# A two-layer graph network on one core: the first round of each half B goes from VectorE to ScalarE, with an accumulator of its own that GpSimd joins

## The chip, the core and the metric

One core of one Trainium2 chip. A core has TensorE (PE: matmuls, with its weight loads, PEld), VectorE (DVE), ScalarE (ACT), GpSimd (POOL) and SyncE (SP), which here only issues DMAs. Each engine works through its own queue in program order and waits on semaphores. PSUM has eight banks of 512 float32 in each of 128 partitions. The metric is the device time of one execution in microseconds; lower is better.

## The reference

128 graphs of 128 nodes with 64 features. Layer 0 is an edge network: for each node the sum over its neighbours of a ReLU of a 192-wide vector, then a 192x64 product. Layer 1 is a message layer with a GRU. Both are residual and end in a layer norm.

```python
def _L0_gnn_ref(x, adj, W1, b1, W2, b2):
    mask = (adj > 0.0)
    W1a, W1b = (W1[:F], W1[F:])
    diff = x[:, :, None, :] - x[:, None, :, :]
    h = relu((x @ W1a)[:, :, None, :] + diff @ W1b + b1)
    hm = jnp.einsum('bjkh,bjk->bjh', h, mask)
    return hm @ W2 + deg[..., None] * b2

x = _layernorm(x + L0(x, adj))
# L1: m = relu(relu(h W1 + b1) W2 + b2); msg = relu(A m); GRU(msg, h)
x = _layernorm(x + L1(x, adj))
```

## The kernel before, in words

**The sum over neighbours.** The adjacency is sparse, so layer 0 is not computed edge by edge over all 128 x 128 pairs. Each node gets its neighbours one after another: in a *round*, TensorE adds into PSUM, for every node of four graphs at once, a matmul with a one-hot matrix (float8 pieces cut out of the bit table `CW`) that swaps the previous neighbour's vector for the next one's. VectorE then reads the three banks, takes the ReLU and adds it to the accumulator `AC`, all in one SCALAR_TENSOR_TENSOR (`max 0, add AC`). The neighbours are in two halves, A (nodes with low numbers, weights `VA`) and B (`VB`). Each half has nine rounds. Rounds 1 to 6 cover 192 columns for each of six tiles (1152 elements), rounds 7 and 8 cover 128 (768 elements), round 9 covers 80 (480 elements). The columns beyond the 128 nodes hold nodes with more neighbours than nine; half A uses the left 64 of them, half B the right 64, and both halves share the middle 128 of one `AC` tile (4 tiles of 128x256 and 2 that hold the rest of the 192 hidden units).

**Turns.** Four graphs make one group `q` (32 groups). In *turn* `t` the program issues, for n from 1 to 9, `round_b(t-1, n)` and then `round_a(t, n)`: half B of the older group alternates with half A of the newer one. Banks 0 to 2 hold even groups, 3 to 5 odd ones, so group t can only be seeded when half B of group t-2 has been read for the last time. So a turn begins with this chain: last B round of group t-2 read by VectorE, `seeds(t)` on TensorE (L836 and L842, it starts PSUM with the node's own term), `seeds(t)` on ScalarE (L1525, ReLU of it into `AC`), `seeds(t)` on GpSimd (L1745, times the number of surplus slots `NNB`), and `round_a(t, 1)` on VectorE, which adds to that `AC` (it waits for `im` and for the cleared outer columns, `clr`).

**The first B round.** `round_b(q, 1)` on TensorE waits for the last A round of group q (`sx`), takes the last A neighbour out again (`leave`, 8 matmuls of 128 columns, L850 and L858) and then adds the first B neighbour (8 matmuls of 192 columns). VectorE reads it like any other round.

**What else the engines do in a turn.** `dgen(t, 0..3)` on VectorE cuts the four one-hot sources `DM[m]` out of `CW` (L1138, 16-bit shifts in SBUF); `words` (L1128) makes the table of the next group; `off` (L1119) every second turn. `prep` (ranks, tables, transposed x, `v`, `surplus` which is ScalarE's `NNB` copy L1513 and L1516), `tail(q)` (`s_ov`, `out0_a`, `out0_b`, `out0_c`: the product with W2 and the residual) and layer 1 (`layer1_steps`) fill TensorE, ScalarE and GpSimd between rounds. GpSimd has the mask (L1698), `gt`, `gt_in`, `gd`, `h` of the GRU (L1640 to L1664), the differences to a float16 copy (L1710 to L1734), the powers of the norms, and `clear` (L1738).

**The order.** The strings `ORDER[t % 2]` (`FIRST` for turn 0, `LAST` for the two last turns) say which step goes between which rounds, for all engines at once: string 2n-1 stands between B round n and A round n, string 2n between A round n and B round n+1, string 0 ahead of B round 1. The letters: `s` seeds, `0` `1` dgen of the next turn, `2` `3` dgen of this turn, `p` prep, `t` tail of group t-2, `r` ranks, `e` `d` `n` layer 1, `c` clear, `l` load. The order within each engine's queue follows from it.

## Time and profile before

| | us |
|---|---|
| three runs | 879.21, 876.65, 873.9 |
| median | 876.65 |
| the profiled execution, its own time | 877.91 |
| span of its trace | 876.3 |
| mean granted TensorE clock | 0.984 of full speed |

Between the span and the execution's own time lie 1.6 us. "Busy" is the union of an engine's instructions. Ends of matmuls are modelled, so that a busy TensorE isn't always one at its peak. "Idle before, released by" is time in which an engine had nothing to run, with the event that ended it. From turn 4 or so to turn 31 the trace repeats itself every two turns within some 0.1 us.

### The profile page before, as it was taken

What the parts mean: (1) busy time and instruction counts of PE and PEld (TensorE: products, weight loads), DVE (VectorE), ACT (ScalarE), POOL (GpSimd) and SP (SyncE); (2) the same over time, 40 slices, a digit from 0 to 9 for tenths busy, and PEclk for the clock granted to TensorE, in tenths of its full rate; (3) what the DMA queues carried; (4) which work ended last, traced back from release to release, by engine and by line L of the source; (5) the groups of instructions that cost most, each with busy time, mean ns of one, the idle gap of its engine ahead of it and who ended that gap; (6) DMA issues with size and microseconds to landing.
All of it is one profiled execution on the core that took longest, in us unless ns stands there. A gap on an engine that the chain in (4) does not pass through costs nothing.

```text
span 876.3 us, 25828 instructions
## 1 busy us (share of the span) xinstructions
PE 786.3 (90%) x10335; PEld 651.6 (74%) x10368; DVE 803.6 (92%) x880; ACT 606.7 (69%) x1863; POOL 462.1 (53%) x536
## 2 busy tenths in 40 slices
PE   3777889999999999999999999999999999999873
PEld 2556677778887787878787787888778787877752
DVE  6799999999999999999999999999999999998961
ACT  4534465777777777777877777787777777776552
POOL 5412243474737547383746647473755738363661
PEclk9998999999999999999999999999999999999996
DMA  3423132322223132313213232312313231221000
GB/s 121 111 46 87 26 92 55 91 54 85 54 65 91 29 104 56 104 32 100 59 33 98 56 103 56 90 46 72 87 27 104 56 104 33 67 56 38 1 13 26
DMA packets 31564, 57.55 MB, mean 66 GB/s; under 512 B 8273, under 2 KB 8913, under 8 KB 31441
## 3 DMA queue, kind: packets, MB, share of 16 engines
q1 hardware_dynamic: 31440, 55.86, 24.5%
q8 instruction: 83, 1.36, 0.6%
q14 instruction: 41, 0.33, 0.1%
HBM read 13.90 MB, written 4.19 MB: 21 GB/s over the span
## 4 chain that ended last, share of the span: by engine, by line
PE 51%; issue 28%; DVE 16%; ACT 2%; POOL 1%; DMA 1%; SPq 1%; POOLq 0%; DVEq 0%
PE PS L850 12%; PE PS L858 11%; DVE AC L1182 8%; DVE AC L1162 4%; PE PS L836 2%; PE PS L932 2%; PE PS L920 2%; PE PS L677 2%; PE PS L842 2%; PE PS L666 2%; PE PS L617 1%; PE PS L618 1%; PE PS L620 1%; PE PS L629 1%; PE PS L627 1%
## 5 line engine op out<-in xcount | busy, mean ns | idle before, releaser
L1182 DVE SCALAR_TENSOR_TENSOR AC<-PS,AC 128x1152 f32<-128x1152 f32 (+2 forms) x279 | 329.4, 1181 | 26.6 <-PE PS L850 25.1
L1162 DVE SCALAR_TENSOR_TENSOR AC<-PS,AC 128x1152 f32<-128x1152 f32 (+2 forms) x279 | 329.4, 1180 | 4.9 <-PE PS L858 2.9
L850 PE MATMUL PS<-DM,VA 128*128 128x192 fp8e5 (+1 forms) x1024 | 121.5, 241 | 17.2 <-DVE AC L1162 11.1
L858 PE MATMUL PS<-DM,VB 128*128 128x192 fp8e5 (+1 forms) x1024 | 120.6, 240 | 17.9 <-DVE AC L1182 15.0
L850 PE MATMUL PS<-DM,VB 128*128 128x192 fp8e5 (+1 forms) x1024 | 119.8, 240 | 0.5 <-DVE AC L1179 0.5
L858 PE MATMUL PS<-DM,VA 128*128 128x192 fp8e5 (+1 forms) x1024 | 120.3, 240 | 0.1
L850 PEld LDWEIGHTS PS<-DM,VA 128*128 128x128 f16 x1024 | 77.7, 99 | 47.8 <-DVE AC L1162 30.4
L1745 POOL TENSOR_TENSOR AC<-AC,NNB 128x512 f32<-128x512 f32 x64 | 66.1, 1053 | 85.7 <-DVE DM L1138 51.4
L858 PEld LDWEIGHTS PS<-DM,VB 128*128 128x128 f16 x1024 | 75.6, 98 | 43.4 <-issue 18.8
L858 PEld LDWEIGHTS PS<-DM,VA 128*128 128x128 f16 x1024 | 83.5, 98 | 0.9 <-DVE AC L1159 0.6
L850 PEld LDWEIGHTS PS<-DM,VB 128*128 128x128 f16 x1024 | 83.4, 98 | 0.9 <-DVE AC L1179 0.9
L1138 DVE TENSOR_SCALAR DM<-CW 128x1536 uint16<-128x1536 uint16 (+1 forms) x132 | 79.2, 628 | 2.5 <-DMA CW<-WM 2.5
L1738 POOL MEMSET AC<- 128x768 f32 x32 | 23.6, 739 | 66.9 <-PE PS L949 66.2
L1698 POOL TENSOR_SCALAR MT<-AT 128x1024 bf16<-128x1024 f32 x15 | 42.1, 2808 | 24.2 <-DMA AT<-in_adjt 23.9
L1734 POOL TENSOR_TENSOR SHL<-SO,SHL 128x256 f16<-128x256 f32 x31 | 28.5, 918 | 49.7 <-ACT SHL L1533 49.7
L1506 ACT ACTIVATE VN<-PS 128x384 f16<-128x384 f32 x64 | 31.2, 487 | 30.5 <-PE PS L815 30.0
L1495 ACT ACTIVATE XE<-PS 128x512 f16<-128x512 f32 x64 | 37.7, 591 | 19.1 <-PE PS L789 19.1
L1501 ACT ACTIVATE VN<-PS 128x384 f16<-128x384 f32 x64 | 31.7, 496 | 20.9 <-PE PS L809 19.3
L1540 ACT ACTIVATE XR<-PS 128x256 f32<-128x256 f32 x32 | 12.3, 384 | 48.5 <-PE PS L949 48.5
L1430 ACT ACTIVATE YO<-Y,st 128x64 f32<-128x64 f32 x120 | 31.8, 337 | 16.3 <-POOL st L1633 16.3
L1475 ACT ACTIVATE AM<-PS 64x512 int16<-64x512 f32 x64 | 37.7, 589 | 6.1 <-PE PS L757 5.7
L1128 DVE TENSOR_TENSOR WM<-c,AM 128x1280 uint16<-128x1280 uint16 x32 | 39.7, 1240 | 2.0 <-ACT OT L1489 2.0
(266 smaller groups left out, 2077.5 us busy)
## 6 DMA issues: line engine op xcount, KB each, us to landing
CW<-WM SPq DMA_DIRECT2D x128, 160.0 KB, 2.8
AT<-in_adjt SPq DMA_DIRECT2D x16, 512.0 KB, 4.9
VA<-VN SPq DMA_DIRECT2D x64, 128.0 KB, 2.3
VB<-VN SPq DMA_DIRECT2D x64, 128.0 KB, 2.3
XN<-in_xn SPq DMA_DIRECT2D x16, 256.0 KB, 4.8
out<-YO SPq DMA_DIRECT2D x15, 256.0 KB, 2.9
cs<-in_cst SPq DMA_DIRECT2D x1, 544.5 KB, 3.4
out<-YO SPq DMA_DIRECT2D x2, 128.0 KB, 1.7
```

The source lines that it names most:

```text
L850: last = e.matmul(PS[:, b + i % 2, 256 * (i // 2) + cols.start:256 * (i // 2) + cols.stop], left(lhs, i), d[:, i, :], start=False, stop=Tr ...
L858: last = e.matmul(PS[:, b + 2, 256 * (i // 2) + cols.start:256 * (i // 2) + cols.stop], right(lhs, i), d[:, i, :], start=False, stop=True, ...
L1128: e.tensor_tensor(WM[q % 2][:], c7[:], AM[q % 2][:].bitcast(U16), ALU.logical_shift_left).then_inc(s["wm"], 1)
L1138: e.tensor_scalar(DM[m][:, halves], CW[t % 3][:, halves, first], 6 - 2 * m, 0xC0C0, ALU.logical_shift_left, ALU.bitwise_and).then_inc(s["d ...
L1162: e.scalar_tensor_tensor(dst, tiles(PS[:, b:b + 3, :])[:, :, cols], 0.0, dst, ALU.max, ALU.add).then_inc(s["sx"], 1)
L1182: e.scalar_tensor_tensor(dst, tiles(PS[:, b:b + 3, :])[:, :, cols], 0.0, dst, ALU.max, ALU.add).then_inc(s["sy"], 1)
L1430: last = e.activation(YO[:, k, :], Y[:, k, :], ACT.Copy, scale=st[:, 3, k:k + 1])
L1475: e.activation(graphs(am[k])[:, :, 64 - 64 * h:192 - 64 * h], src[k], ACT.Copy, scale=2.0, bias=-258.0)
L1495: e.activation(XE[q % 4][:, 2 * k:2 * k + 2, :].rearrange("p i n -> p (i n)"), PS[:, b, :], ACT.Copy).then_inc(s["xe"], 1)
L1501: e.activation(VN[q % 2][:, 0, k:4:2, 0:H], PS[:, b, :].rearrange("p (a n) -> p a n", a=2)[:, :, 0:H], ACT.Copy).then_inc(s["vh"], 1)
L1698: e.tensor_scalar(MT[g % 3][:], AT[g % NA][:], 0.0, None, ALU.is_gt).then_inc(s["mask"], 1)
L1745: e.tensor_tensor(t[:, h, nat], t[:, h, nat], NNB[q % 2][:, h, :], ALU.mult).then_inc(s["im"], 1)
```

## The change

1. VectorE no longer does `round_b(q, 1)`. ScalarE does: one ACTIVATE Relu over the 1152 elements (two, of 384 and 768, for the last group), which *writes* an accumulator of half B of its own, `BB[q % 2]`. VectorE's B rounds 2 to 9 add to `BB`. One `BB` is new memory, the other lies over the constants that are not needed after the start (`cs`, whose `CSL` column moves forward for that).
2. GpSimd gets `join(q)`: two TENSOR_TENSOR adds (128x512 and 128x256 float32) of the middle columns of `BB` to `AC`, as the first step of `tail(q)`. It waits for both halves' ninth round; `out0_a` on TensorE waits for it.
3. `clear` writes 128x384 instead of 128x768, since half B's outer columns are written and not added to.
4. `VA` has two buffers instead of three; SP's `v_out(q)` waits for the first B round of group q-2 on TensorE.
5. The tables `ORDER`, `FIRST` and `LAST` are drawn anew. Around the start of a turn the order is then:

```
even turn, before: B9 A9 dgen0 dgen1 surplus seeds dgen2 ov B1 rank_t A1 rank_ov gt_in dgen3 tanh gd B2
even turn, after:  gt_in dgen1 surplus rank_n A9 seeds ov tanh B1 gd dgen2 dgen3 A1 join rank_t h rank_ov B2
                   (dgen0 three rounds earlier, between A6 and B7)
odd turn, before:  B9 dgen0 A9 off dgen1 surplus seeds dgen2 B1 ov dgen3 m2 rank_t A1 s_ov B2 A2 msg split_ms B3
odd turn, after:   B9 dgen0 dgen1 A9 off surplus seeds B1 dgen2 msg split_ms A1 B2 ov gate_h gate_i dgen3 rank_t A2 join B3
```

```diff
-    ("s2p", "p", "pe3ee", "td", "erp", "t", "tt", "rpr", "p", "ed", "p", "epree", "pee", "d", "pce", "", "", "0", "r1"),
-    ("s2", "p3dp", "t", "", "d", "p", "eptp", "e", "ptl", "tp", "ndcpn", "d", "p", "dr", "pnd", "", "dd", "d", "01p"),
+    ("spe", "e23", "tpep", "", "tp", "rdd", "tp", "t", "ept", "rp", "erepe", "d", "p", "epce", "d", "", "de", "01", "r"),
+    ("s", "2d", "", "pdd3p", "t", "te", "p", "tp", "tt", "ndnl", "drc", "pp", "dd0p", "", "pp", "p", "d", "d1per", ""),
...
-        VA = [sb(f"VA{i}", [128, 4, 256], F16) for i in range(3)]
+        VA = [sb(f"VA{i}", [128, 4, 256], F16) for i in range(2)]
...
-        AC = [sb(f"AC{i}", [128, 3, 512]) for i in range(3)]
+        AC = [sb(f"AC{i}", [128, 6, H]) for i in range(3)]
+        BB = [sb("BB0", [128, 6, H])[:], cs[:, CTR:CTR + 6 * H].rearrange("p (k n) -> p k n", k=6)]
...
             def tail(q):
+                do("join", q)
+                yield
...
             def out0_a(q, b, gates):
-                pe.wait_ge(s["sy"], 9 * q + 9)
+                pe.wait_ge(s["jn"], 2 * q + 2)
```

On VectorE:

```diff
             def round_b(q, n):
+                if n == 1:
+                    return
```

On ScalarE:

```diff
+            def round_b(q, n):
+                if n > 1:
+                    return
+                b, dst = 3 * (q % 2), BB[q % 2]
+                ac.wait_ge(s["jn"], 2 * (q - 2) + 2)
+                ac.wait_ge(s["sov"], q - 1)
...
+                ac.wait_ge(s["gy"], 9 * q + 1)
+                e.activation(dst, tiles(PS[:, b:b + 3, :])[:, :, back], ACT.Relu).then_inc(s["sy"], 1)
```

On GpSimd, and at the end on SP:

```diff
+            def join(q):
+                po.wait_ge(s["sx"], 9 * q + 9)
+                po.wait_ge(s["sy"], 9 * q + 9)
+                for h in (slice(0, 4), slice(4, 6)):
+                    t = AC[q % 3][:, h, nat]
+                    e.tensor_tensor(t, t, BB[q % 2][:, h, 0:128], ALU.add).then_inc(s["jn"], 1)
...
             def clear(q):
                 po.wait_ge(s["o0"], q - 2)
-                e.memset(outer(tiles(AC[q % 3][:])), 0.0).then_inc(s["clr"], 1)
+                e.memset(AC[q % 3][:, :, 0:64], 0.0).then_inc(s["clr"], 1)
...
             def v_out(q):
+                sy.wait_ge(s["gy"], 9 * (q - 2) + 1)
```

## Rows read from the trace of the kernel before

**Rows 1.** The page: busy time of each engine over the span.
```profile
PE 786.3 (90%) x10335; PEld 651.6 (74%) x10368; DVE 803.6 (92%) x880; ACT 606.7 (69%) x1863; POOL 462.1 (53%) x536
```
**Rows 2.** Busy time by stretch: an even turn, then an odd one.
```profile
423.69:448.34 24.65, 22.74 (x316) 19.11 (x316) 24.65 (x25) 19.31 (x61) 18.19 (x25) 1.00 0.21 50
448.34:473.65 25.31, 25.15 (x331) 20.95 (x332) 23.47 (x25) 18.78 (x58) 11.20 (x10) 1.00 0.33 90
```
**Rows 3.** Groups by line and form: busy us, mean ns of one, idle before.
```profile
L1182 DVE SCALAR_TENSOR_TENSOR AC<-PS,AC 128x1152 f32<-128x1152 f32 x186 | 250.8, 1348 | 23.3 <-PE PS L850 21.9
...
L1745 POOL TENSOR_TENSOR AC<-AC,NNB 128x512 f32<-128x512 f32 x32 | 43.9, 1372 | 85.7 <-DVE DM L1138 51.4 <-ACT AC L1525 34.3
...
L1495 ACT ACTIVATE XE<-PS 128x512 f16<-128x512 f32 x64 | 37.7, 591 | 19.1 <-PE PS L789 19.1
...
L1516 ACT ACTIVATE NNB<-PS 64x256 f32<-64x256 f32 x64 | 23.9, 373 | 0.4
...
L1745 POOL TENSOR_TENSOR AC<-AC,NNB 128x256 f32<-128x256 f32 x32 | 23.5, 733 | 0.0
```
**Rows 4.** VectorE in order of time (start, us) around an even turn's start.
```profile
419.89 0.65 DVE L1182 SCALAR_TENSOR_TENSOR AC<-PS,AC 128x480 f32<-128x480 f32 x1
...
421.18 1.51 DVE L1138 TENSOR_SCALAR DM<-CW 128x1536 uint16<-128x1536 uint16 x3
423.69 1.36 DVE L1182 SCALAR_TENSOR_TENSOR AC<-PS,AC 128x1152 f32<-128x1152 f32 x1 [0.99 <-PE PS L850]
424.97 1.36 DVE L1162 SCALAR_TENSOR_TENSOR AC<-PS,AC 128x1152 f32<-128x1152 f32 x1
426.24 0.55 DVE L1138 TENSOR_SCALAR DM<-CW 128x1536 uint16<-128x1536 uint16 x1
426.71 1.35 DVE L1182 SCALAR_TENSOR_TENSOR AC<-PS,AC 128x1152 f32<-128x1152 f32 x1
```
**Rows 5.** TensorE in order of time at the same place: seeds, leave, B1.
```profile
420.63 0.60 PE L836 MATMUL PS<-XE,wxh 128*128 128x256 f16 x4
...
421.83 0.39 PE L842 MATMUL PS<-XE,wxl 128*64 128x256 f16 x4
422.38 0.39 PE L850 MATMUL PS<-CW,VA 128*128 128x128 fp8e5 x4 [0.16 <-DVE DM L1138]
...
423.16 0.49 PE L850 MATMUL PS<-DM,VB 128*128 128x192 fp8e5 x4
```
**Rows 6.** ScalarE in order of time at the same place.
```profile
422.10 0.87 ACT L1525 ACTIVATE AC<-PS 128x512 f32<-128x512 f32 x2
422.86 0.69 ACT L1465 ACTIVATE OV<-PS,cs 128x512 bf16<-128x512 f32 x1
```
**Rows 7.** GpSimd in order of time at the same place.
```profile
417.30 2.79 POOL L1698 TENSOR_SCALAR MT<-AT 128x1024 bf16<-128x1024 f32 x1 [1.00 <-DMA AT<-in_adjt]
...
422.87 1.96 POOL L1745 TENSOR_TENSOR AC<-AC,NNB 128x512 f32<-128x512 f32 x2 [1.53 <-ACT AC L1525]
```
**Rows 8.** VectorE in order of time around the next odd turn's start.
```profile
444.64 0.64 DVE L1182 SCALAR_TENSOR_TENSOR AC<-PS,AC 128x480 f32<-128x480 f32 x1
...
449.61 1.04 DVE L1138 TENSOR_SCALAR DM<-CW 128x1536 uint16<-128x1536 uint16 x1
450.57 1.34 DVE L1162 SCALAR_TENSOR_TENSOR AC<-PS,AC 128x1152 f32<-128x1152 f32 x1
452.28 1.36 DVE L1182 SCALAR_TENSOR_TENSOR AC<-PS,AC 128x1152 f32<-128x1152 f32 x1 [0.36 <-PE PS L850]
```
**Rows 9.** GpSimd in order of time at that odd turn's start.
```profile
448.08 2.15 POOL L1745 TENSOR_TENSOR AC<-AC,NNB 128x512 f32<-128x512 f32 x2 [2.71 <-DVE DM L1138]
```
**Rows 10.** One line's instructions (min/median/max ns): VectorE's words.
```profile
L1128 DVE TENSOR_TENSOR WM<-c,AM x32: 810/815/1921, 19.8 to 779.3; 128x1280 uint16<-128x1280 uint16 x32
```
**Rows 11.** VectorE's words and GpSimd beside it, in order of time.
```profile
429.24 1.90 DVE L1128 TENSOR_TENSOR WM<-c,AM 128x1280 uint16<-128x1280 uint16 x1
...
429.18 1.27 POOL L1656 TENSOR_TENSOR GT<-GT,GZ 128x512 f32<-128x512 f32 x1
```

More of the change, by code:

```diff
@@ L46 @@
 CI = 0
-CTR = CI + 128
+CSL = CI + 128
+CTR = CSL + 1
 CTX = CTR + 128
@@ L293, in build @@
         ident = cs[:, CI:CI + 128]
+        ACD = [t[:].rearrange("p (a b) n -> p a (b n)", b=2) for t in AC]
         nat, front, back = slice(64, 192), slice(0, 192), slice(64, 256)
@@ L885, in round_a @@
                     pe.wait_ge(s["sx"], 9 * q + n - 1)
-                last = wide(q, VA[q % 3][:], d, cols)
+                last = wide(q, VA[q % 2][:], d, cols)
                 if q == 0:
@@ L896, in round_b @@
                     leave = lasts(q, 0, 0)
-                    wide(q, VA[q % 3][:], leave, nat)
-                    padded(q, VA[q % 3][:], leave, nat)
+                    wide(q, VA[q % 2][:], leave, nat)
+                    padded(q, VA[q % 2][:], leave, nat)
                 elif q == NQ - 1:
@@ L1562, in scalar_main @@
             follow(main_order, {"rank_n": rank_n, "split_x": split_x, "off": off, "ov": ov, "rank_t": rank_t, "rank_ov": rank_ov,
-                                "x_turn": x_turn, "v": v, "v_low": v_low, "surplus": surplus, "seeds": seeds, "s_ov": s_ov, "out0_c": out0_c,
+                                "x_turn": x_turn, "v": v, "v_low": v_low, "surplus": surplus, "seeds": seeds, "round_b": round_b, "s_ov": s_ov, "out0_c": out0_c,
                                 "fold": fold, "split_x1": split_x1, "split_h": split_h,
@@ L1750, in dgen @@
                     po.wait_ge(s["dd"], RD * t + m + 1)
-            follow(main_order, {"setup": setup, "parts": parts, "count": count, "split_x": split_x, "mask": mask, "split_xg": split_xg, "split_ms": split_ms, "split_x1": split_x1, "split_h": split_h, "s_ov": s_ov, "clear": clear, "seeds": seeds, "dgen": dgen, **gpsimd_layer1(e, po, s)})
+            follow(main_order, {"setup": setup, "parts": parts, "count": count, "split_x": split_x, "mask": mask, "split_xg": split_xg, "split_ms": split_ms, "split_x1": split_x1, "split_h": split_h, "s_ov": s_ov, "join": join, "clear": clear, "seeds": seeds, "dgen": dgen, **gpsimd_layer1(e, po, s)})
         def gpsimd_dense(e):
```

62 lines of the change are left out of this document (31 added, 31 removed), and 2 rows, old and new, of the table MAIN.

## The prediction

> **What bounds the kernel now.** I read the page first: VectorE is busy for 803.6 of 876.3 us, TensorE for 786.3, ScalarE for 606.7, GpSimd for 462.1 [rows 1]. Then the busy time of one even and one odd turn, since the trace repeats in pairs of turns. In the even turn VectorE has no idle time at all in 24.65 us; in the odd one it is busy for 23.47 of 25.31 us, while TensorE is busy for 25.15 [rows 2]. A pair takes 49.96 us, of which VectorE idles 1.84. So VectorE is the bound by its share, with TensorE close behind, and the instruction that the change takes away is one of its costliest: a round of 1152 elements, 1348 ns each [rows 3]. They overlap a little: in order of time the next one starts 1.27 to 1.28 us later [rows 4].
>
> A share doesn't say what the removal is worth. I therefore read the start of a turn in order of time, engine by engine. Call X the end of the last B round of the turn before. At the even turn X is 420.54 (419.89 + 0.65). TensorE starts the seeds at 420.63, because they need the banks that this round read [rows 5]; their last group starts at 421.83 and has 0.24 to go, and the 8 leave matmuls start at 422.38, the first B round ends its issue by 423.5. ScalarE turns the seeds into `AC` from 422.10 on, in 0.87 [rows 6]. GpSimd multiplies them from 422.87 for 1.96, until 424.83 [rows 7]. Only then may VectorE add A round 1, and it does at 424.97 [rows 4], X + 4.43. So B round 1 (423.69) stands in a gap that VectorE has anyway: the seed chain X, TensorE, ScalarE, GpSimd, A round 1 takes nearly as long without it. That is what the reader is to see: 24.65 of 24.65 busy, and yet a chain beside it that is as long as the work.
>
> At the odd turn X is 445.28 (444.64 + 0.64). GpSimd multiplies from 448.08 for 2.15 [rows 9], A round 1 starts at 450.57, X + 5.29, and B round 2 at 452.28, X + 7.00, after 0.36 of idle [rows 8]. Here the chain frees A round 1 at 450.23, X + 4.95.
>
> **The change part by part.** The paying case: 31 groups by 1.27 us is 39 us. Now what the chain leaves of it.
>
> *Even turn.* Before, B round 2 starts at X + 6.17 (426.71) [rows 4]. After, dgen 0 has left this stretch for the middle of the turn before (it will cost 0.47 there, the step from 426.24 to 426.71), and dgen 1 to 3 (3 x 0.5) and A round 9 end at about X + 2.0. Then VectorE waits for the multiplied seeds. They come at X + 4.3 if nothing moves, at about X + 4.1 if ScalarE, now done with its `NNB` copies ahead of the turn, starts them 0.3 earlier: the seeds' first half is through TensorE by X + 1.2. A round 1 then ends 1.27 later at X + 5.4. The other chain is the new one: seeds end X + 1.55, ov 0.2, leave and B1 1.1, ScalarE, then B round 2 on TensorE, 0.66 for its 8 matmuls and some 0.2 to be seen. ScalarE's read of 1152 elements isn't in the trace. Bounds: not under the 0.59 of 512 elements and, by the step from 256 (373 ns) to 512 (591 ns, both [rows 3]), 0.85 ns an element, so 1.14; at most the 1.35 that VectorE takes. I take 1.14, as the same engine's slope is the nearest row. Ahead of it in ScalarE's queue stand ov (0.69 [rows 6]) and tanh. So B round 2 is ready at about X + 5.5, and starts there: 0.67 earlier than before, less the 0.47 of dgen 0, a gain of 0.2. If ScalarE is late by half a microsecond, it is a loss of 0.3.
>
> *Odd turn.* dgen 0 and 1, A round 9, `off` and dgen 2 end near X + 3.1. The multiplied seeds come at X + 4.7 (GpSimd free of a dgen) to X + 4.95 (as now), B round 2 is 1.27 later, X + 6.0 to 6.2 against 7.00. But dgen 3, ahead of A round 1 before, now follows B round 2: 0.47, and more if GpSimd is in its way. So the gain is 0.3 to 0.5 without that wait.
>
> *GpSimd's work.* Join costs GpSimd 1.37 + 0.73 = 2.1 us a turn, by the same forms [rows 3]; half of a clear is given back. It is hidden where nobody waits: `out0_a` comes slots later. The cost lies elsewhere. words on VectorE takes 815 ns as a median and 1921 at most [rows 10]; the one of 1.90 started at 429.24, 0.06 after a GpSimd TENSOR_TENSOR of 1.27 (429.18), and had to let it end [rows 11]. dgen does so too: 1.04 beside GpSimd's second multiplication [rows 8], 0.55 alone [rows 4]. In the new odd turn `split_ms` and join stand on GpSimd just where dgen 3 is issued (seeds end X + 4.7, then 1.2 and 2.1): a wait of 0 to 1.27. I take 0.3. In the even turn words keeps a wait; its place moves, so that it costs between nothing and 1.27, before 1.09; I take 0.4 less.
> The page SBUF — State Buffer of the Trainium skill, section "SBUF: two separate sides", says that VectorE's fast forms and GpSimd share one pair of ports as an exclusive lock for a whole instruction, and the other "fully blocks". The 1.90 against 0.81 agrees; by that rule every join is a new chance for a block, and if each dgen and words met one of 0.65 the pair would lose some 3 us more, while the rounds themselves, which read PSUM, would not be touched.
>
> *Sum.* A pair gains 0.2 + 0.4 (even) and 0.4 - 0.3 (odd), 0.7 us. Turns 1 to 4 are longer by other waits; taking 15 pairs, 10.5 us. At the end of the kernel join is uncovered: nothing but the last group's product follows, so 2.1 less what runs beside it (`s_ov` and its copies), 1.5 us lost. `VA`'s new wait is free: TensorE's first B round comes at the start of the turn in which v_out is issued. 877.9 - 10.5 + 1.5 = 868.9 against the profiled execution, which is 1.26 above the median; so 868 against the median of 876.65.
>
> **The rivals.**
> *Full pay* (11%). VectorE's share decides and the tables fill the gap with other work: 31 x 1.27 = 39 us, or 30 with the end and some waits, 838 to 855. For it: no idle in the even turn. Against: the seed chain stands in the trace with its own length, and the steps that could fill the gap (dgen 0) were moved away from it.
> *Chain and TensorE eat all* (27%). The gap stays as long as it was, and in the odd turn TensorE, 25.15 of 25.31 busy, gives nothing; 0.2 to 0.3 a pair. 872.3 to 881.
> *GpSimd's queue holds the seeds* (20%). The slower side: before the even turn GpSimd runs the mask, 417.30 to 420.09, and is then free until 422.87 [rows 7] but for `gt`. The new order also puts `gt_in` (1.27, the size of row L1656 [rows 11]) ahead of the seeds' multiplication, and dgen 1 to 3 fight with it. The mask waits for a DMA, so it can't start sooner; a turn shorter by a microsecond moves X towards it. From the point at which mask, gt and gt_in (5.3 us from 417.3 on, so 422.6) end later than X + 2.0, each microsecond is one of the turn. At 0.5 to 1 us for an even turn beyond the gain, and dgen 3's full wait of 0.65 in the odd one, the pair loses 0.3 to 0.9: 881 to 892.
> That the change doesn't do what it says (ScalarE always late, so that A and B rounds lose their alternation) is the far end of the same side.
>
> **How the numbers follow.** Forecast 42%, between 855 and 872.3, likeliest 868. Full pay 11%, nothing 27%, slower 20%. 80% is reached from 852 to 884. 0.5% (4.4 us) is about what a measurement of this kernel can tell from no change. Faster by over 0.5% (under 872.3) 0.53, within 0.27, slower 0.20.
>
> **What the profile after would show.** B round 1 gone from VectorE's line and an ACTIVATE of 128x1152 at about 1.14 us. At an even turn's start VectorE idle for some 2 us, released by GpSimd's multiplication; at an odd one 1.6. B round 2 released by TensorE at X + 5.5. A pair near 49.3. words still with cases of 1.6 to 1.9, dgen more often over 1.0. If VectorE idles less than 1 us a turn and is busy about 39 us less, full pay was right. If GpSimd's L1745 group starts later than X + 2.6 in even turns, the slower rival is. The prediction falls if ScalarE's read starts far later than TensorE's B round 1 ends, or if the middle of the turns changes length by more than the two dgens.

## Result, and the profile after

| | before | after |
|---|---|---|
| median of 8 runs each, us | 876.35 | 882.83 (879.77 to 886.61) |
| after / before | | 1.0069, 95% interval 1.0048 to 1.009 |
| profiled execution, us | 877.91 | 882.54 |
| its span | 876.3 | 880.7 |
| mean granted TensorE clock | 0.984 | 0.984 |

The change made the kernel slower by 0.7%. The time was forecast at 868, faster; 882.8 lies in the range, on the other side. Ratios here and below are of runs with the chip in its faster state; one run of the second experiment was in the slower state, and its median counts it.

The page of the changed kernel, busy time of each engine (against [rows 1]):

```profile
PE 801.0 (91%) x10368; PEld 654.4 (74%) x10368; DVE 770.5 (87%) x847; ACT 643.8 (73%) x1896; POOL 520.0 (59%) x600
```

VectorE did lose its work: 803.6 became 770.5, 33 us less. ScalarE got 37 more, GpSimd 58. (TensorE, whose work is the same, reads 801.0 for 786.3; 33 of its records are missing in the trace before and its ends are modelled, so nothing is built on that.) The time didn't follow VectorE. Two turns in stretches from A round 1 to A round 1, the first mostly turn 16, an even one, the second turn 17 (columns as in [rows 2]):

```profile
426.15:451.02 24.87, 24.34 (x341) 21.02 (x342) 22.54 (x22) 21.68 (x68) 19.25 (x25) 1.00 0.21 50
451.02:475.84 24.82, 24.51 (x325) 19.48 (x323) 22.62 (x23) 18.73 (x55) 13.87 (x13) 1.00 0.34 91
```

VectorE, without any idle time in the even turn before [rows 2], now idles 2.3 us of 24.9 and 2.2 of 24.8; TensorE is at 24.3 and 24.5. Where VectorE waits, by line (busy, mean ns of one, idle before, releaser), with the groups that the change touches:

```profile
L1162 DVE SCALAR_TENSOR_TENSOR AC<-PS,AC 128x1152 f32<-128x1152 f32 x186 | 251.2, 1350 | 47.4 <-POOL AC L1767 40.9 <-PE PS L858 6.3
...
L1138 DVE TENSOR_SCALAR DM<-CW 128x1536 uint16<-128x1536 uint16 (+1 forms) x132 | 96.1, 749 | 2.9 <-DMA CW<-WM 2.9
...
L1767 POOL TENSOR_TENSOR AC<-AC,NNB 128x512 f32<-128x512 f32 x32 | 49.6, 1549 | 75.4 <-ACT AC L1524 70.1 <-DVE DM L1138 5.1
...
L1756 POOL TENSOR_TENSOR AC<-AC,BB 128x512 f32<-128x512 f32 x16 | 20.4, 1278 | 2.2 <-DVE DM L1138 2.2
```

The wait is at one place. VectorE in order of time at the start of turn 18, an even one (compare [rows 4]), and GpSimd beside it:

```profile
470.60 0.66 DVE L1181 SCALAR_TENSOR_TENSOR BB<-PS,BB 128x480 f32<-128x480 f32 x1
471.17 0.72 DVE L1138 TENSOR_SCALAR DM<-CW 128x1536 uint16<-128x1536 uint16 x1
471.81 0.64 DVE L1162 SCALAR_TENSOR_TENSOR AC<-PS,AC 128x480 f32<-128x480 f32 x1
472.37 1.52 DVE L1138 TENSOR_SCALAR DM<-CW 128x1536 uint16<-128x1536 uint16 x2
475.84 1.36 DVE L1162 SCALAR_TENSOR_TENSOR AC<-PS,AC 128x1152 f32<-128x1152 f32 x1 [1.94 <-POOL AC L1767]
477.11 1.35 DVE L1181 SCALAR_TENSOR_TENSOR cs<-PS,cs 128x1152 f32<-128x1152 f32 x1
```

```profile
470.20 1.27 POOL L1655 TENSOR_TENSOR GT<-GT,GR 128x512 f32<-128x512 f32 x1
471.64 1.38 POOL L1662 TENSOR_TENSOR GT<-GT,M 128x512 f32<-128x512 f32 x1 [0.17 <-POOL GT L1655]
473.44 2.27 POOL L1767 TENSOR_TENSOR AC<-AC,NNB 128x512 f32<-128x512 f32 x2 [0.42 <-DVE DM L1138]
```

The gap that B round 1 filled is now there to be seen: X is 471.25, A round 1 starts at X + 4.59, 1.94 of it idle. Worked out for turns 6 to 29 from VectorE's rows (12 pairs of turns; us per pair but for the first line):

| | before | after |
|---|---|---|
| one turn | 24.995 | 25.106 |
| rounds of 1152 elements | 24, 32.4 | 22, 29.7 |
| dgen, 8 | 5.00 | 6.13 |
| words, 2 | 2.67 | 2.08 |
| VectorE idle | 1.82 | 3.98 |

The rounds lost 2.6 a pair. 2.16 of idle time and 1.13 of slower dgens came back, less 0.60 of faster words. By place, with each instruction counted until the next one starts (means of the same 12 pairs, after less before, us):

| stretch | length | rounds | dgen and words | idle |
|---|---|---|---|---|
| even turn, X to B round 2 | 0.00 | -1.28 | +0.91 | +0.37 |
| even turn, the rest | +0.03 | +0.28 | -0.60 | +0.35 |
| odd turn, X to B round 2 | -0.68 | -1.34 | -0.94 | +1.58 |
| odd turn, the rest | +0.87 | -0.14 | +1.15 | -0.14 |

So the steady turns come out nearly even: the last group's B round 9 ends at 843.13 before and 843.37 after. The other 4.2 us of the span are behind it: 33.1 us from there to the end before, 37.4 after. These are single traces. A second trace of the same steady turns (the first run on the last stretch, below) has turns of 25.05 and the last round at 839.17, so 0.06 a turn, and some 4 us in the place of the last round, are not told from none. The stretch behind the last round is firmer: 33.1 to 33.3 in four traces of kernels with the structure and tables of before.

### The profile page after: what moved, and what is told of

Its sections match the earlier page's. It is cut to its first block, busy times and chain, and to the rows that moved or that the text cites. A ratio compares the mean times of both kernels' runs of the same rounds, so it can differ in the third digit from the quotient of the medians.

```text
span 880.7 us, 26002 instructions
## 1 busy us (share of the span) xinstructions
PE 801.0 (91%) x10368; PEld 654.4 (74%) x10368; DVE 770.5 (87%) x847; ACT 643.8 (73%) x1896; POOL 520.0 (59%) x600
## 3 DMA queue, kind: packets, MB, share of 16 engines
q1 hardware_dynamic: 31440, 55.86, 24.5%
## 4 chain that ended last, share of the span: by engine, by line
PE 50%; issue 17%; DVE 9%; POOL 7%; ACT 3%; DMA 1%; SPq 1%; POOLq 0%; DVEq 0%; ACTq 0%
PE PS L850 12%; PE PS L858 11%; DVE AC L1162 4%; DVE cs L1181 3%; PE PS L920 2%; PE PS L932 2%; POOL AC L1767 2%; PE PS L677 2%; PE PS L942 2%; PE PS L836 2%; PE PS L666 2%; DMA VB<-VN 1%; PE PS L939 1%; PE PS L620 1%; PE PS L618 1%
## 5 line engine op out<-in xcount | busy, mean ns | idle before, releaser
L1162 DVE SCALAR_TENSOR_TENSOR AC<-PS,AC 128x1152 f32<-128x1152 f32 (+2 forms) x279 | 329.9, 1183 | 47.7 <-POOL AC L1767 40.9
L1181 DVE SCALAR_TENSOR_TENSOR BB<-PS,BB 128x1152 f32<-128x1152 f32 (+2 forms) x128 | 149.0, 1164 | 4.0 <-PE PS L850 3.1
L1181 DVE SCALAR_TENSOR_TENSOR cs<-PS,cs 128x1152 f32<-128x1152 f32 (+1 forms) x120 | 139.6, 1163 | 6.7 <-PE PS L850 5.5
L1767 POOL TENSOR_TENSOR AC<-AC,NNB 128x512 f32<-128x512 f32 x64 | 74.9, 1189 | 75.4 <-ACT AC L1524 70.1
L1138 DVE TENSOR_SCALAR DM<-CW 128x1536 uint16<-128x1536 uint16 (+1 forms) x132 | 96.1, 749 | 2.9 <-DMA CW<-WM 2.9
L1713 POOL TENSOR_SCALAR MT<-AT 128x1024 bf16<-128x1024 f32 x15 | 43.5, 2900 | 40.9 <-DMA AT<-in_adjt 40.9
L1494 ACT ACTIVATE XE<-PS 128x512 f16<-128x512 f32 x64 | 36.1, 592 | 22.0 <-PE PS L789 22.0
L1505 ACT ACTIVATE VN<-PS 128x384 f16<-128x384 f32 x64 | 31.1, 486 | 27.1 <-PE PS L815 27.1
L1756 POOL TENSOR_TENSOR AC<-AC,cs 128x512 f32<-128x512 f32 (+1 forms) x32 | 27.4, 879 | 27.4 <-DVE DM L1138 27.3
L932 PE MATMUL PS<-w2s,AC 128*128 128x64 f32 x256 | 40.1, 289 | 0.0
L920 PE MATMUL PS<-w2s,AC 128*64 128x64 f32 x512 | 38.2, 231 | 0.0
L920 PEld LDWEIGHTS PS<-w2s,AC 128*64 128x64 f32 x512 | 33.7, 143 | 5.4 <-issue 3.8
```

The lines of the kernel that those rows point to most:

```text
L920: last = e.matmul(PS[64 * h:64 * h + 64, b, 64 * i:64 * i + 64], lhs, w2s[:, w, :], start=(w == 0), stop=(w > 0))
L932: e.matmul(o, ac[:, 2 * (i % 2) + i // 2, nat], w2s[:, 0, :], start=False, stop=True, skip_group_check=True)
L1138: e.tensor_scalar(DM[m][:, halves], CW[t % 3][:, halves, first], 6 - 2 * m, 0xC0C0, ALU.logical_shift_left, ALU.bitwise_and).then_inc(s["d ...
L1162: e.scalar_tensor_tensor(dst, tiles(PS[:, b:b + 3, :])[:, :, cols], 0.0, dst, ALU.max, ALU.add).then_inc(s["sx"], 1)
L1181: e.scalar_tensor_tensor(dst, tiles(PS[:, b:b + 3, :])[:, :, cols], 0.0, dst, ALU.max, ALU.add).then_inc(s["sy"], 1)
L1494: e.activation(XE[q % 4][:, 2 * k:2 * k + 2, :].rearrange("p i n -> p (i n)"), PS[:, b, :], ACT.Copy).then_inc(s["xe"], 1)
```

## Experiments

Ratios are to runs of the kernel before that were taken beside each experiment. "Idle" is VectorE's, us per pair of turns, worked out as above; a turn's length likewise. 

**Are the tables or the structure to blame?** First the changed kernel with all three tables of before, join right behind the seeds:

```diff
-    ("spe", "e23", "tpep", "", "tp", "rdd", "tp", "t", "ept", "rp", "erepe", "d", "p", "epce", "d", "", "de", "01", "r"),
+    ("s2p", "p", "pe3ee", "td", "erp", "t", "tt", "rpr", "p", "ed", "p", "epree", "pee", "d", "pce", "", "", "0", "r1"),
...
             def tail(q):
-                do("join", q)
-                yield
```

> The change's structure (first B round on ScalarE, own accumulator, join on GpSimd, two VA buffers) with the tables of before; join follows the seeds' multiplication at once. If the seed chain at the turn's start (last B round, TensorE, ScalarE, GpSimd, A round 1) is the reason that nothing was gained, A round 1 still starts 4.3 to 4.5 us after the last B round in even turns and near 5 in odd ones, and the time is 872 to 880. If the new tables are what spoilt the change, it is 865 or less: the removed 1.27 us a turn then shows.

Measured: 900.81, ratio 1.0288 [1.0257, 1.0319], far above the numbers of both theories; a turn 25.60, idle 5.09, A round 1 at X + 4.41 (even) and 5.87 (odd). In the even turn, with the order of before and without B round 1, A round 1 starts where it did before (4.43): this is the plainest proof that the round stood in a gap. The gap tells nothing of the rest of the turn, which grew. VectorE's waits over the run (line waited for: us, times, longest):

```profile
DVE AC L1165 <- POOL AC L1770: 33.8, 17, 2.3
DVE AC L1165 <- PE PS L861: 23.7, 30, 3.0
DVE BB L1184 <- PE PS L853: 12.3, 29, 2.1
```

Then the other half, the kernel before with only the strings of the new tables:

> The kernel before with the new tables alone; the first B round stays on VectorE, and there is no join. If the removed round only filled a gap that the seed chain leaves anyway, putting it back costs little: 880 to 888, with VectorE's wait for GpSimd's multiplication gone from about 2 us to under 1. If VectorE's work sets the time of the changed kernel, the round costs 31 x 1.27 = 39 us: about 920.

Measured: 930.45, ratio 1.0591 [1.0538, 1.0645]; a turn 26.52. Here A round 1 of even turns waits behind B round 1 and starts at X + 7.28: `DVE AC L1183 <- PE PS L851` is 49.9 us of waits. Each order is worth its time with its own structure alone. By the ratios: structure with old tables +25 us, tables with old structure +52, both +6. The new tables took back three quarters of what the structure costs in the old order.

**What join costs.** The changed kernel without it (the middle columns of half B are missing from the result):

```diff
             def tail(q):
-                do("join", q)
...
-                pe.wait_ge(s["jn"], 2 * q + 2)
+                pe.wait_ge(s["sx"], 9 * q + 9)
+                pe.wait_ge(s["sy"], 9 * q + 9)
...
-                ac.wait_ge(s["jn"], 2 * (q - 2) + 2)
```

> The changed kernel without the join: the middle columns of half B are left out of the result; out0_a waits for both halves' ninth round directly. Seed chain: join is no part of it, so 876 to 882, of which 1.5 to 3 at the end of the kernel. If GpSimd's extra 2.1 us a turn (and VectorE's short instructions waiting for it) is the cause, 868 or less.

Measured: 878.28, ratio 1.0022 [0.9996, 1.0047]; a turn 25.00, dgen 5.80, words 1.82, idle 4.28. Join is worth some 4 us (give or take 3, by the intervals). dgen and words are 0.6 a pair cheaper without it. The last stretch took 36.1 for 37.4, but that is not shown to be join's: see the end of the next part. Without join the body is as long as before, no shorter. GpSimd's busy time is back at 461.3, the 462.1 of before, and dgen keeps 0.80 of the 1.13 that the change had added: which of GpSimd's work stands beside a dgen counts for more than how much work it has.

**Is it GpSimd's multiplication?** The same kernel with the seeds not multiplied (a factor is missing), so that A round 1 waits for ScalarE's copy:

```diff
             def round_a(q, n):
-                    ve.wait_ge(s["im"], 2 * q + 2)
+                    ve.wait_ge(s["ini"], 2 * q + 2)
...
-                    e.tensor_tensor(t[:, h, nat], t[:, h, nat], NNB[q % 2][:, h, :], ALU.mult).then_inc(s["im"], 1)
```

> The changed kernel without the multiplication of the seeds on GpSimd (the surplus factor is left out of the result); A round 1 waits for ScalarE's copy of the seeds alone. Seed chain: A round 1 moves up by about 1.5 us a turn to where TensorE's A round 1 lets it start, 835 to 860. If GpSimd were not in the chain and TensorE or the middle of the turn set the time, 875 to 883.

Measured: 879.26, ratio 1.0023 [1.0002, 1.0044]; a turn 25.08, idle 4.08, A round 1 at X + 4.28 as a mean of even turns for 4.88, and 4.74 for 5.05 in odd ones. VectorE's largest wait, in the changed kernel and in this one:

```profile
DVE AC L1162 <- POOL AC L1767: 40.9, 26, 2.1
```

```profile
DVE AC L1162 <- PE PS L858: 48.3, 31, 3.0
```

The wait has the same place and about the same size, and another releaser. A chain of TensorE's (seeds, leave, B round 1, then A round 1 in its queue) stands nearly as late as GpSimd's, and the turn didn't get shorter by what A round 1 gained.

**The dgen that was moved away.** dgen 0 of odd turns goes back to the turn's end, as before the change:

```diff
-    ("s", "2d", "", "pdd3p", "t", "te", "p", "tp", "tt", "ndnl", "drc", "pp", "dd0p", "", "pp", "p", "d", "d1per", ""),
+    ("s", "2d", "", "pdd3p", "t", "te", "p", "tp", "tt", "ndnl", "drc", "pp", "ddp", "", "pp", "p", "d", "d01per", ""),
```

> The changed kernel with one step moved in its tables: the even turn's first dgen goes back from between A round 6 and B round 7 of the turn before to behind its last B round, so that it may fill VectorE's wait at the turn's start. If that wait is free room, 0.47 us are saved in every second turn: 7 us, 874 to 877. If the dgen, there, makes GpSimd's multiplication of the seeds later (GpSimd is held until it is done) or A round 9, the gain is eaten: 880 to 887.

Measured: 882.15, ratio 1.0044 [1.0024, 1.0064]; a turn 25.09, idle 3.01 and dgen 7.16. Idle time fell by 0.97 a pair and dgen rose by 1.03 (3.00 and 7.27 in a second trace with the same order): the gap can be filled, but what fills it stands beside GpSimd's work and takes the time that it frees.

**Seeds ahead of `gt_in`.** On top of the last one, `gt_in`, `tanh` and `gd` of even turns go behind B round 1 (the letter `d` of `gt_in` leaves the odd string):

```diff
-    ("spe", "e23", "tpep", "", "tp", "rdd", "tp", "t", "ept", "rp", "erepe", "d", "p", "epce", "d", "", "de", "01", "r"),
+    ("sp", "eee23", "tpep", "", "tp", "rdd", "tp", "t", "ept", "rp", "erepe", "d", "p", "epce", "d", "", "de", "01", "r"),
-    ("s", "2d", "", "pdd3p", "t", "te", "p", "tp", "tt", "ndnl", "drc", "pp", "ddp", "", "pp", "p", "d", "d01per", ""),
+    ("s", "2d", "", "pdd3p", "t", "te", "p", "tp", "tt", "ndnl", "drc", "pp", "ddp", "", "pp", "p", "d", "01per", ""),
```

> As the run with dgen 0 moved back, and gt_in, tanh and gd put behind the first B round, so that GpSimd multiplies the seeds first in even turns. If GpSimd's queue is what makes the seeds late there (4.6 to 6.1 us after the last B round, 4.1 by the sum), A round 1 starts at 4.1 to 4.4 in all even turns: 870 to 876. If TensorE's seeds, leave, B and A round in a row are as late, 878 to 883.

Measured: 897.34, ratio 1.0241 [1.0181, 1.03]; a turn 25.77, idle 5.79, dgen down to 5.08. dgen is nearly at its price of before, and A round 1 comes at X + 4.38 to 4.41 in 5 of 12 even turns; but those turns take 26.2. words waits for a copy of ScalarE's:

```profile
DVE WM L1128 <- ACT OT L1488: 14.7, 13, 2.3
```

**Another way to free A round 1.** The seeds go into half B's accumulator (three of them), ScalarE reads A round 1, VectorE B round 1; then the multiplication is needed a round later. Once with the new tables, once with those of before but for a few steps:

```diff
-                    e.activation(AC[q % 3][:, h, nat], tiles(PS[:, b:b + 3, :])[:, h, nat], ACT.Relu).then_inc(s["ini"], 1)
+                    e.activation(BB[q % 3][:, h, 0:128], tiles(PS[:, b:b + 3, :])[:, h, nat], ACT.Relu).then_inc(s["ini"], 1)
...
-            def round_b(q, n):
+            def round_a(q, n):
```

> The other way round: the seeds go into half B's accumulator (three of them), ScalarE writes half A's accumulator in A round 1, and B round 1 stays on VectorE, where the seeds are due a whole turn later. Everything else, the tables too, as in the changed kernel. ScalarE's and VectorE's loads are the same as in the changed kernel. If the wait for the multiplied seeds is what ate the 39 us, it goes: VectorE's wait for GpSimd's multiplication is 0, and the time is 860 to 872. If the tables and TensorE's row of seeds, B1 and A1 set the turn, 878 to 895.

> The same exchange with the tables of before, in which only the steps between B round 1 and A round 1 that would keep ScalarE from A round 1 (rank_t, m2) are moved behind it, and the join is ahead of the seeds on GpSimd. VectorE then goes from B round 1 at 2.4 to 3.1 us after the last B round to B round 2 at 5.1, against 6.2 and 7.0 before: 850 to 866 if the seed chain was the cause. If TensorE is the bound in the turns with much layer 1 work, 868 to 880.

Measured: 901.19, ratio 1.0287 [1.025, 1.0324], and 905.6, ratio 1.0312 [1.0274, 1.0349]; 25.71 and 25.79 a turn. The wait for GpSimd is gone from both, and waits for TensorE's rounds stand in its place (19.1, 15.1 and 13.4 us in the first). In the second, TensorE, VectorE and ScalarE in order of time:

```profile
406.35 1.05 PE L671 MATMUL PS<-BD,M 128*128 128x128 f32 x8
...
408.09 0.27 PE L925 MATMUL PS<-w2s,AC 128*64 128x64 f32 x1 [0.47 <-ACT M L1373]
```

```profile
405.53 1.35 DVE L1186 SCALAR_TENSOR_TENSOR XB<-PS,XB 128x1152 f32<-128x1152 f32 x1
406.80 0.78 DVE L1143 TENSOR_SCALAR DM<-CW 128x1536 uint16<-128x1536 uint16 x1
410.05 1.36 DVE L1186 SCALAR_TENSOR_TENSOR XB<-PS,XB 128x1152 f32<-128x1152 f32 x1 [2.47 <-PE PS L855]
```

```profile
406.34 1.13 ACT L1546 ACTIVATE AC<-PS 128x1152 f32<-128x1152 f32 x1
407.44 0.60 ACT L1373 ACTIVATE M<-PS 128x512 f32<-128x512 f32 x1
```

`s_ov` on TensorE (L925) waits 0.47 for ScalarE's copy `M`, then takes some 1.1; B round 2 is queued behind it, and VectorE waits 2.47. ScalarE's read of the round, 1.13, stands ahead of that copy, but isn't what made it late: the product it copies (L671) ends at 407.40 and the read at 407.47. So TensorE's own filling steps between two rounds are what VectorE waits for here, and no price of ScalarE's round is shown.

**The last stretch.** The changed kernel with join and `s_ov` in one step for the last group; then the same with dgen 0 put back:

```diff
                 do("join", q)
-                yield
+                if q < NQ - 1:
+                    yield
```

> The changed kernel with one thing altered: for the last group the join and s_ov stand in one step, so that layer 1's steps no longer come between them in the order of the last stretch. If the 4.2 us of the measured difference that lie behind the last B round come from s_ov being moved behind layer 1 on TensorE, the stretch from the last B round to the end falls from 37.4 to 33 to 35 us and the time to 878 to 880. If they come from the join itself (GpSimd, 1.7 us, and out0_a waiting for it), 881 to 883.

> The same with dgen 0 moved back, whose trace had its last B round 2.4 us before that of the kernel before: if both effects add, 875 to 878, level with the kernel before; no more, since nothing here shortens the start of a turn. If they don't add, 879 to 882.

Measured: 883.17, ratio 1.0085 [1.0065, 1.0105], and 881.96, ratio 1.0066 [1.0041, 1.0091]. From the last B round to the end it took 38.0 and 38.1 us, not the 33 to 35 expected. That one step between join and `s_ov` isn't what makes the end longer. The other traces say more. The rows of the first 8 us behind the last round (as in [rows 2], the seventh number is the granted clock), the changed kernel and then the run with `gt_in` behind B round 1, which has the same last tables and join:

```profile
843.37:851.37 8.00, 7.34 (x81) 5.54 (x78) 0.68 (x3) 2.99 (x8) 2.81 (x4) 0.67 0.01 2
860.13:868.13 8.00, 6.72 (x96) 5.13 (x96) 1.54 (x7) 4.46 (x18) 2.84 (x4) 1.00 0.01 2
```

All traces with the changed structure and the last tables as drawn (with join unless said):

| run | granted clock in these 8 us | last round to end, us |
|---|---|---|
| `gt_in` behind B round 1 | 1.00 | 34.7 |
| without multiplication and join, `msg` later (next part) | 1.00 | 34.9 |
| without multiplication, `msg` later (next part) | 0.84 | 36.1 |
| VectorE's cut (below) | 0.83 | 36.1 |
| without join | 0.83 | 36.1 |
| dgen 0 back | 0.75 | 37.1 |
| seeds in half B, new tables | 0.75 | 36.9 |
| TensorE's cuts, one or both (below) | 0.75, 0.69 | 36.6, 36.0 |
| changed kernel | 0.67 | 37.4 |
| without multiplication | 0.50 | 39.5 |

The kernel before has 1.00 there and takes 33.1. At the same clock the stretch is as long with join as without (36.1 and 36.1, 34.7 and 34.9), so join adds nothing there that shows; the runs of each pair differ in another cut too, but in none of the last group's work behind the last round. The length goes with the clock in the main. At a clock of 1.00 the changed order costs 1.6 us at the end, and the changed kernel's remaining 2.7 go with the lower clock. What lowers it in one trace and not in another isn't known.

**An earlier A round 1.** Without the multiplication, and with `msg` of odd turns behind A round 1; then without join as well:

```diff
-    ("s", "2d", "", "pdd3p", "t", "te", "p", "tp", "tt", "ndnl", "drc", "pp", "dd0p", "", "pp", "p", "d", "d1per", ""),
+    ("s", "2", "d", "pdd3p", "t", "te", "p", "tp", "tt", "ndnl", "drc", "pp", "dd0p", "", "pp", "p", "d", "d1per", ""),
```

> The run without the multiplication of the seeds, with msg in odd turns moved behind A round 1 too: both chains that end at A round 1 are cut. If those two chains, equally long, are what ate the removed round, A round 1 of odd turns starts at 3.7 to 4.0 us instead of 4.74, and the last B round comes 10 to 15 us earlier: 864 to 872. If TensorE's order and its banks set the turn anyway, as the even turns of 24.9 suggest, the odd turn keeps its 25.2 and the time is 877 to 882.

> The same without the join: GpSimd then has no part in the new work or the seeds. The middle columns of half B and the surplus factor are left out of the result. If GpSimd's instructions stretch VectorE's dgen and words, a further 4 us go (as between the changed kernel and the one without the join): 860 to 868, or 873 to 878 if the rival of the run before holds.

Measured: 886.87, ratio 1.0116 [1.0091, 1.0142], and 883.4, ratio 1.0098 [1.0071, 1.0125]. A round 1 of odd turns came at X + 3.70, against 5.05 in the changed kernel, and the odd turn took 25.87 for 25.28 (medians). The earliest A round 1 of all made one of the longest odd turns. `msg` moved too, so this isn't the chain's effect alone; but the chain at a turn's start, on which the prediction was built, doesn't set the turn by itself.

**Which engine does?** Four runs cut a known amount of one engine's work and leave all waits. TensorE's cut leaves out the float32 products of `AC` in `out0_a` and `out0_b`; VectorE's lets rounds 7 and 8 read half their columns. Each was done to both kernels:

```diff
-                    e.matmul(o, ac[:, 2 * (i % 2) + i // 2, nat], w2s[:, 0, :], start=False, stop=True,
-                             skip_group_check=True)
...
-                for k in range(2):
-                    e.matmul(PS[:, b, 128 * k:128 * k + 128], ac[:, 4 + k, nat],
-                             w2s[:, 1:3, :].rearrange("p k n -> p (k n)"), start=False, stop=True, skip_group_check=True)
```

```diff
                 cols = front if n <= C1 else nat if n < C0 else ninth
+                if n in (7, 8) and 0 < q < NQ - 1:
+                    cols = slice(64, 128)
```

> The changed kernel with the float32 products of AC with W2 left out of TensorE's tail steps (4 matmuls of 128x64 in out0_a, 2 of 128x128 in out0_b; the output lacks these terms). In the trace of the changed kernel they take the steps from 408.10 to 408.35 four times and from 410.20 to 410.73, so 4 x 0.25 + 0.53 = 1.5 us of TensorE a turn, all in the middle of turns; all waits stay. Theory 'chain and VectorE': a turn is the chain up to A round 1 (4.6 to 5.1) and then VectorE's own work (idle 0.65 a pair); TensorE's fillers decide nothing, so the time stays within 875 to 884, idle of VectorE stays near 4 us a pair. Theory 'TensorE': its queue, 97% busy, sets the turns since the round has left VectorE; then 1.0 to 1.5 us a turn goes, 838 to 852, and VectorE idles under 2 us a pair.

> The kernel before with the same six float32 matmuls a group left out (same part of the output missing). Before, VectorE has no idle time in the even turn and 1.84 in the odd one. Theory 'chain and VectorE': at most the odd turn's wait goes, 0.5 a pair or less, 869 to 877. Theory 'TensorE': VectorE bounds before in even turns, but TensorE in odd ones; at most the 1.84 of a pair goes, 848 to 869, less than in the changed kernel.

> The changed kernel with VectorE's rounds 7 and 8 of both halves reading only 64 of their 128 columns (384 elements for 768, groups 1 to 30; the sum lacks the other columns' terms). 945 ns fall to some 550, so 4 x 0.4 = 1.6 us of VectorE a pair; TensorE's and all other work stays. Theory 'chain and VectorE': it is gone in full, 15 x 1.6 = 24 us, 855 to 862, idle stays near 4.0 a pair. Theory 'TensorE': nothing or little goes, 876 to 884, and VectorE's idle grows to 5.5 a pair, released by TensorE.

> The kernel before with the same half columns in rounds 7 and 8. By both theories VectorE bounds the even turns, where it never idles: 0.8 of the even turn goes. In the odd turn TensorE was busy for 25.15 of 25.31: theory 'TensorE' gives nothing there (862 to 867), theory 'chain and VectorE' gives 0.8 there too (851 to 856).

The cut of VectorE was twice what these texts say: 8 rounds a pair are halved, not 4, so 3.2 us. Then both cuts at once, in each kernel:

> The changed kernel with both cuts at once: the six float32 matmuls of a group (1.5 us of TensorE a turn) and half the columns of rounds 7 and 8 (which measured 3.2 us of VectorE a pair, 8 rounds of 0.4, not the 1.6 put down for the two runs before). The same parts of the output are missing. Alone, TensorE's cut of 3.1 a pair gave back 0.47 a pair and VectorE's of 3.2 gave 0.26. Theory 'TensorE and VectorE are level': each cut was held back by the other engine, so both together give 2.4 to 3.1 a pair, 36 to 47 us beyond the changed kernel: 836 to 847. Theory 'a third': the chain at the turn's start (X, seeds, ScalarE, GpSimd, A round 1) and the alternation of the rounds through ScalarE and GpSimd hold the turn; then the two together give no more than their sum and a little, 0.7 to 1.2 a pair, 862 to 872.

> The kernel before with both cuts. Alone, TensorE's gave nothing (25.00 to 25.03 a turn) and VectorE's 3.2 a pair gave 0.44. Theory 'level': both together 2.4 to 3.1 a pair, 829 to 841. Theory 'a third': 0.5 to 1.0 a pair, 861 to 870. If this kernel gains much more by both cuts than the changed one, the third thing is in what the change added (chain without cover, join).

Measured. The first columns are busy time against the same kernel uncut, from the pages; the gain is the difference of the ratios to before, times 877:

| kernel and cut | TensorE busy | VectorE busy | us | ratio, interval | gain, us |
|---|---|---|---|---|---|
| after, TensorE | -32.4 | -5.1 | 870.27 | 0.9914 [0.9888, 0.9939] | 13.6 |
| before, TensorE | -33.6 | -1.7 | 875.7 | 0.9974 [0.9946, 1.0002] | 2.3 |
| after, VectorE | -6.1 | -37.7 | 877.54 | 1.0005 [0.9989, 1.0021] | 5.6 |
| before, VectorE | +2.0 | -42.5 | 865.45 | 0.9872 [0.9833, 0.9911] | 11.2 |
| after, both | -45.7 | -37.1 | 866.21 | 0.9892 [0.9856, 0.9929] | 15.5 |
| before, both | -42.3 | -42.1 | 864.67 | 0.9873 [0.9838, 0.9908] | 11.1 |

The page's first line of the changed kernel with VectorE's cut, then with TensorE's:

```profile
PE 794.9 (91%) x10368; PEld 651.8 (75%) x10368; DVE 732.8 (84%) x847; ACT 644.8 (74%) x1896; POOL 518.7 (59%) x600
```

```profile
PE 768.6 (88%) x9984; PEld 609.3 (70%) x9984; DVE 765.4 (88%) x847; ACT 643.7 (74%) x1896; POOL 517.9 (60%) x600
```

Three things follow. First, in the kernel before VectorE's time was worth about a quarter of itself (11.2 for 42.5) and TensorE's nothing that can be told from none. Second, the change moved the limit: after it, VectorE's time is worth a seventh (5.6 for 37.7) and TensorE's two fifths (13.6 for 32.4). Third, neither engine alone holds the turn, nor do the two together: with both cuts (some 33 us of TensorE's work, its busy time reads lower by 46 and 42 with 46 and 33 records missing, and 37 to 42 of VectorE's) both kernels end within 0.2% of each other, at 24.77 and 24.73 us a turn, and gain no more than 16. With VectorE's cut the changed kernel's waits move to B rounds:

```profile
DVE cs L1185 <- PE PS L850: 24.1, 33, 1.1
DVE AC L1164 <- PE PS L858: 14.9, 34, 2.8
DVE BB L1185 <- PE PS L850: 13.5, 43, 0.4
```

Its idle time is 6.23 a pair against 3.98, its dgens 6.46 against 6.13: of the 3.2 us that were taken out, 2.25 came back as idle time, mostly waits for TensorE, 0.3 as slower dgens, and 0.26 were gained; the rest is in overlaps. In the kernel before with both cuts the chain that ended last goes, once a pair, through layer 1's norm on the other two engines (start, us):

```profile
431.20 1.41 ACT SY L1420 x12
...
433.47 1.87 POOL st L1632
...
435.61 0.81 ACT YO L1429 x3
```

What holds the 24.7 us turn isn't settled by these runs. Of GpSimd's work, 59 us (join) and 76 us (the multiplication, 520.0 to 444.4 busy) were cut and gave some 4 us each. ScalarE's was not cut in any run; its share is seen only in such chains and waits.

## Why the prediction was wrong, point by point

**B round 1 fills a gap that VectorE has anyway: right.** Its removal left VectorE idle for 1.94 us at an even turn's start, released by GpSimd's multiplication, as the prediction said (2 us, and 40.9 in all), and with the order of before A round 1 didn't move when it went (4.41 for 4.43). That holds for the order of before; in the new one the round does not fit back in (the run at 1.0591). ScalarE's read of 1152 elements was estimated at 1.14 from the slope of [rows 3]; it takes 1.12:

```profile
474.71 1.12 ACT L1540 ACTIVATE cs<-PS 128x1152 f32<-128x1152 f32 x1
```

**The even turn, A round 1 at about X + 4.1 and B round 2 at X + 5.5, a gain of 0.2: wrong, and the step that failed.** A round 1 came at X + 4.6 to 4.8 in 8 of 12 turns and later in the others, 4.88 as a mean for 4.49 before. B round 2 came at 6.23 as a mean, and 6.23 before: nothing was gained for the round and the dgen 0 that had both left this stretch. The step is "if ScalarE, now done with its `NNB` copies ahead of the turn, starts them 0.3 earlier". It was not done with them. ScalarE in order of time, where X is 471.25:

```profile
470.82 0.60 ACT L1512 ACTIVATE NNB<-PS 128x512 f32<-128x512 f32 x1
471.31 0.76 ACT L1515 ACTIVATE NNB<-PS 64x256 f32<-64x256 f32 x2
472.09 0.69 ACT L1443 ACTIVATE Q<-PS,cs 128x512 bf16<-128x512 f32 x1
472.68 0.90 ACT L1524 ACTIVATE AC<-PS 128x512 f32<-128x512 f32 x2
```

The `NNB` copies ended at X + 0.8, then came `rank_n`'s copy `Q`, which the new order puts there, and the seeds' copy began at X + 1.43, 0.13 earlier than the 1.56 of before. So the multiplication started at X + 2.19 (473.44 - 471.25), 0.14 earlier, but took 2.27 for the 1.96 of [rows 7]: its first instruction ran 1.59 beside a dgen, 1.27 without one. The 0.42 of idle time before it is put down to a dgen in the row above, but it ended with ScalarE's copy, whose first half ends at 473.27: GpSimd's waits for dgens 2 and 3 (`po.wait_ge(s["dd"], RD * t + m + 1)`, L1772) stand behind the multiplication in its queue, and in turn 8 it started at X + 2.18 while dgen 2 ran until X + 2.54.

**The odd turn, A round 1 at X + 4.7 to 4.95, B round 2 at 6.0 to 6.2: the direction right, the size off.** Measured 5.05 and 6.32, a gain of 0.68 against 7.00 [rows 8], before dgen 3. The multiplication started at X + 2.59, 0.22 earlier than before, no longer behind a dgen, and lost most of that by running 1.64 for 1.47.

**dgen 3's wait of 0.3: in the wrong place and too small. words 0.4 less: right.** words gave 0.60 a pair. But the 8 dgens went from 5.00 to 6.13, where the sum had 0.3 for one. That one, dgen 3 of the odd turn, took 0.55 in all 12 turns and was never held. The stretched ones stand around the even turn's start, beside `gt`, `gt_in` and the multiplication, where the new order put GpSimd's work: dgen 1 took 0.71 to 1.55, and of dgens 2 and 3 one or both took 1.05 to 1.08 or 1.62 in every turn (in the rows above, 1.05 at 472.37, while GpSimd's L1662 ran from 471.64 to 473.02). GpSimd's 58 us more of busy time are not the cause by themselves: without join, at 461.3 busy, the dgens cost 5.80, and without the multiplication, at 444.4, 5.43, both more than the 5.00 of before at 462.1; with the new tables alone, at 455.5, they cost 7.24, and the structure with the old tables, at 515.1, 5.91. What counts is which of GpSimd's work stands beside a dgen, more than how much there is. By the rule cited from the Trainium skill (page SBUF — State Buffer, section "SBUF: two separate sides") a dgen or words that meets an instruction of GpSimd's which started first is blocked until that one ends. The prediction's case of it was mis-summed: ten instructions of a pair by 0.65 are 6.5 us, not 3. 0.5 was measured (1.13 - 0.60), since 31 of 96 dgens ran longer than 0.6 us (13 of 96 before), and words were held less than before.

**The pair at 49.3: wrong, 50.2.** The terms 0.2 + 0.4 + 0.4 - 0.3 = 0.7 became -0.2. The even turn's start gave 0.0, the odd one's 0.68; the rest of the odd turn took 0.87 (dgens 0 and 3, which went there, 1.15), and words' 0.60 went to idle time and rounds in the rest of the even turn. The experiments show that their common premise was too simple as well. The prediction followed one chain from X to B round 2 and took the rest of the turn for VectorE's own work, of fixed length. In the run with A round 1 at X + 3.7 the rest grew by 1.9 us (22.16 from A round 1 to the next X against 20.24). And of 42.5 us less VectorE work outside the turn's start, the kernel before gave back 11.2. At that rate, an estimate from a cut in another place, the removed 33 us were worth about 9 (33 x 11.2 / 42.5), before any cost; the full-pay rival (39 us, 11%) was further from it than it seemed.

**The end loses 1.5: mis-sized, 4.2, and for another reason.** This is nearly the whole difference of the spans (4.4). The 1.5 was to be join's; join adds nothing that shows. In the kernel before `s_ov` of the last group ran at 840.39, ahead of the last round's end, and the residual `XR` was read at 846.55. In the changed one it is at 845.14, behind layer 1's steps, and `XR` follows at 851.80. TensorE of both kernels in this stretch (busy as in [rows 2], the seventh number is the granted clock, of full speed); before first:

```profile
843.10:851.00 7.90, 6.25 (x66) 4.65 (x66) 2.56 (x10) 3.50 (x14) 3.93 (x5) 1.00 0.01 2
```

```profile
843.40:852.00 8.60, 7.95 (x90) 6.01 (x86) 0.68 (x3) 3.20 (x9) 2.81 (x3) 0.70 0.01 2
```

VectorE and ScalarE of the changed kernel there:

```profile
848.22 0.42 DVE L1228 TENSOR_TENSOR SHL<-SO,SHL 128x256 f16<-128x256 f32 x1 [4.85 <-ACT SHL L1548]
```

```profile
851.80 0.38 ACT L1555 ACTIVATE XR<-PS 128x256 f32<-128x256 f32 x1 [0.51 <-PE PS L949]
```

More matmuls fall behind the last round, and in part at the lower of TensorE's two clock levels, which before shows only later. By the table of the last stretch, 1.6 us are the order's (34.7 for 33.1, both at a clock of 1.00 in the first 8 us) and 2.7 go with the clock (37.4 at 0.67). Putting `s_ov` beside join gave nothing back (38.0).

**The rivals.** Full pay: refuted, VectorE was busy 33 us less and idle 37 more. "Chain and TensorE eat all" named what happened to the turns, an eaten gain, and gave 872 to 881; the result is above it by the end stretch. "GpSimd's queue holds the seeds" gave the time best (881 to 892), and its mechanism is there in one turn. Turn 10, GpSimd and then VectorE:

```profile
266.99 2.79 POOL L1713 TENSOR_SCALAR MT<-AT 128x1024 bf16<-128x1024 f32 x1 [3.41 <-DMA AT<-in_adjt]
...
270.52 1.27 POOL L1655 TENSOR_TENSOR GT<-GT,GR 128x512 f32<-128x512 f32 x1
271.96 1.37 POOL L1662 TENSOR_TENSOR GT<-GT,M 128x512 f32<-128x512 f32 x1 [0.17 <-POOL GT L1655]
273.30 2.27 POOL L1767 TENSOR_TENSOR AC<-AC,NNB 128x512 f32<-128x512 f32 x2
```

```profile
271.13 2.62 DVE L1138 TENSOR_SCALAR DM<-CW 128x1536 uint16<-128x1536 uint16 x2
275.69 1.36 DVE L1162 SCALAR_TENSOR_TENSOR AC<-PS,AC 128x1152 f32<-128x1152 f32 x1 [1.94 <-POOL AC L1767]
```

The mask waits for its DMA, `gt_in` ends late, the multiplication starts at X + 3.76 (X is 269.54), past the X + 2.6 that the prediction set as the sign, and the turn takes 25.97 for the 24.4 to 24.6 of 7 others. But this is the only one of 12 even turns past that sign, and without the multiplication the time was 4 us less only. So that rival was right in its sign and its place, and is a small part of the cause.

No run beat the kernel before, among those that compute the whole result.
